# Adding b2 with the residual load of a decoder layer's feed-forward, in place of products with ones

## The reference, cut to what matters

```
def _quant_per_tensor(x):
    scale = jnp.maximum(jnp.max(jnp.abs(x)), MIN_RANGE) / QP
    return (_ste_round(x / scale), scale)

def _qlinear(x2d, w, b):
    xq, sx = _quant_per_tensor(x2d)
    wq, sw = _quant_per_tensor(w)
    out = jnp.matmul(xq, wq.T) + b[None, :]
    return out * (sw * sx)

h = _qlinear(x.reshape(-1, D), w1, b1)
h = jax.nn.gelu(h, approximate=False)
o = _qlinear(h, w2, b2)
x = x + o
```

## Time and profile before

| what | us |
|---|---|
| median of 3 runs | 1654.87 |
| lowest and highest | 1651.92, 1656.31 |
| profiled execution, its own time | 1657.15 |
| its span, first to last instruction | 1655.3 |
| second pass: scale of h known, to the last add_residual's start | 1549.5 to 1650.55 |

### The profile page before, as it was taken

How to read it: one execution, slowest core, us unless ns; L and a number is a source line. 1 busy time by engine, 2 the same in 40 slices (tenths; PEclk the granted TensorE clock), 3 DMA queues, 4 the chain that set the end, 5 groups by cost and what they waited for, 6 DMA issues and landing times.

```text
span 1655.3 us, 52293 instructions
## 1 busy us (share of the span) xinstructions
PE 1546.7 (93%) x15938; PEld 1228.1 (74%) x15946; DVE 1460.6 (88%) x6188; ACT 1216.4 (73%) x2497; POOL 1074.7 (65%) x1168
## 2 busy tenths in 40 slices
PE   6689999999999999999999999999999999779897
PEld 5568888888888788888888888888888887542465
DVE  4779999999999999999999999999999997669876
ACT  4767777777777777777777777777777776469875
POOL 3467777777777777777777777777777777642000
PEclk9789999999999999999999999999999999889999
DMA  6000000000000000000000000000000000246154
GB/s 213 1 18 29 29 29 29 29 26 24 27 29 29 29 29 29 29 22 23 26 29 26 24 29 29 29 29 29 29 29 29 29 29 17 90 103 151 39 178 166
DMA packets 92292, 74.67 MB, mean 45 GB/s; under 512 B 20832, under 2 KB 91744, under 8 KB 92256
## 3 DMA queue, kind: packets, MB, share of 16 engines
q1 hardware_dynamic: 91296, 74.08, 14.5%
q10 hardware_dynamic: 960, 0.13, 0.1%
HBM read 45.36 MB, written 25.17 MB: 43 GB/s over the span
## 4 chain that ended last, share of the span: by engine, by line
PE 40%; DVE 35%; issue 12%; ACT 6%; DMA 3%; POOL 2%; DVEq 1%; SPq 1%; ACTq 0%; POOLq 0%
PE banks L124 10%; PE banks L127 8%; PE banks L128 8%; DVE scores L1379 6%; DVE tile_max L2118 4%; PE banks L906 3%; DVE sparse_in L1450 3%; DVE heads_t_half L1401 2%; PE banks L926 2%; DVE xn L1334 2%; DMA x_in<-in_x_dram 2%; DVE left L1431 2%; PE banks L798 2%; PE banks L2022 2%; DVE g_t_half L1355 2%
## 5 line engine op out<-in xcount | busy, mean ns | idle before, releaser
L646 POOL TENSOR_TENSOR shifted<-scores,score_max 128x512 f32<-128x512 f32 x256 | 266.8, 1048 | 200.4 <-DVE score_max L1379 195.7
L652 POOL TENSOR_TENSOR exp_t<-exp_copy,exp_t 128x512 f16<-128x512 f32 x256 | 303.9, 1187 | 81.0 <-ACT exp_copy L1168 78.5
L1379 DVE CUSTOM_DVE_ANT_0 scores<-banks,mask 128x128 f32<-128x128 f32 x1024 | 232.7, 285 | 6.5 <-PE banks L906 2.9
L638 POOL TENSOR_TENSOR v_nat<-kv_copy,v_nat 128x512 f16<-128x512 f32 x128 | 149.3, 1167 | 44.4 <-ACT kv_copy L1146 44.4
L1143 ACT ACTIVATE q_t<-banks 128x512 f16<-128x512 f32 x128 | 77.1, 603 | 131.4 <-PE banks L128 131.1
L926 PE MATMUL banks<-ident,shifted 128*128 128x128 f32 x1024 | 153.6, 278 | 10.5 <-ACT exp_copy L1168 6.9
L1166 ACT ACTIVATE exp_t<-banks 128x512 f16<-128x512 f32 x256 | 152.6, 596 | 5.7 <-PE banks L116 2.9
L1168 ACT ACTIVATE exp_copy<-banks 128x512 f32<-128x512 f32 x256 | 155.3, 607 | 0.0
L1146 ACT ACTIVATE kv_copy<-banks 128x512 f32<-128x512 f32 x252 | 149.8, 595 | 0.0
L638 POOL TENSOR_TENSOR k_t<-kv_copy,k_t 128x512 f16<-128x512 f32 x124 | 144.2, 1163 | 0.0
L114 PE MATMUL banks<-v_nat,exp_t 128*128 128x66 f16 x1024 | 121.9, 195 | 7.9 <-POOL exp_t L652 3.2
(11 more groups left out here) (276 smaller groups left out, 5117.4 us busy)
## 6 DMA issues: line engine op xcount, KB each, us to landing
x_in<-in_x_dram SPq DMA_DIRECT2D x32, 256.0 KB, 2.7
ctx_in<-in_ctx_dram SPq DMA_DIRECT2D x32, 256.0 KB, 2.6
x_residual<-x SPq DMA_DIRECT2D x64, 128.0 KB, 1.7
x_normalised<-normed SPq DMA_DIRECT2D x32, 256.0 KB, 2.1
shared<-x_normalised SPq DMA_DIRECT2D x8, 1024.0 KB, 7.0
shared<-x_residual SPq DMA_DIRECT2D x16, 512.0 KB, 3.7
out_dram<-shared SPq DMA_DIRECT2D x16, 512.0 KB, 2.9
mask<-in_fside_Bx1xSxS_dram SPq DMA_DIRECT2D x64, 64.0 KB, 2.0
```

Source lines behind the costliest of these rows:

```text
L638: pool.tensor_tensor(hilo(dst, *at)[LO], src, hilo(dst, *at)[HI], ALU.subtract).then_inc(kv_split, 1)
L646: pool.tensor_tensor(shifted[:, q % 2], scores[:, q % 2], score_max[:, q % 2, :].unsqueeze(2).to_broadcast([P, QUAD, P]), ALU.subtract).th ...
L652: pool.tensor_tensor(exp_t[:, q % 2, LO], exp_copy[:, q % 2], exp_t[:, q % 2, HI], ALU.subtract).then_inc(exp_split, 1)
L1379: op = dve.tensor_tensor_reduce(scores[:, q % 2, h, :], sc_bank(q)[:, tile(h)], mask[:, b, :], 1.0, NEG, ALU.add, ALU.max, score_max[:, q ...
```

## The change

`split_b2`, the tensors `ones` and `b2_parts`, and the 32 matmuls of L2028 are removed. The last product of each slice in a half closes the sum, and VectorE waits for `stepped` in place of `acc_full`. GpSimd computes `b2_scaled` = b2 * s once, after the scale of h is known. `reload(n)` on SyncE's queue no longer loads the residual: it copies `b2_scaled` into the four places of the slot, from SBUF to SBUF. When that has landed (`b2_put`), GpSimd's queue issues the load of the residual with `accum_op=ALU.add`, so the slot then holds x2 + b2 * s, and this load's landing is what `again_loaded` counts. The transfer reads the slot, adds, and writes it.

```
-            if back and not front:
-                ffn_of["split_b2"](pool)
...
-    b2_parts = sb("b2_parts", [P, 2, D], BF16)
-    ones = sb("f_ones", [P, P], BF16)
+    b2_scaled = sb("b2_scaled", [P, D])
...
         def reload(n):
-            sp.dma_start(x_again[:, n % 2], x2_halves[half_of(n)]).then_inc(again_loaded[n % 2], 16)
-
-        sp.wait_ge(b2_ready, 3)
+
+            sp.dma_start(x_again[:, n % 2], b2_scaled[:].unsqueeze(1).to_broadcast([P, HB, D])).then_inc(b2_put[n % 2], 16)
+
+        sp.wait_ge(b2_ready, 1)
         reload(0)
         reload(1)
...
+        half_of = lambda n: 2 * SEQUENCE[n // 2] + n % 2
+        pool.wait_ge(b2_loaded, 16)
+        pool.wait_ge(scale_step, 6)
+        pool.tensor_scalar(b2_scaled[:], keep["b2_row"][:], both[:, 1:2], None, ALU.mult).then_inc(b2_ready, 1)
+        for n in range(HALVES):
+            pool.wait_ge(b2_put[n % 2], 16 * (n // 2 + 1))
+            pool.dma_start(x_again[:, n % 2], x2_halves[half_of(n)], accum_op=ALU.add).then_inc(again_loaded[n % 2], 16)
...
-                               keep["w2_q"][:, t, :], start=(t == 0 and b % 2 == 0), stop=False, skip_group_check=True)
+                               keep["w2_q"][:, t, :], start=(t == 0 and b % 2 == 0), stop=(t == ET - 1), skip_group_check=True)
             mm.then_inc(stepped, 1)
-            if t == ET - 1:
-                for b in (0, 2):
-                    mm = pe.matmul(acc_bank(half, b), ones[:], b2_parts[:].rearrange("p n d -> p (n d)"),
-                                   start=False, stop=True, skip_group_check=True)
-                mm.then_inc(acc_full, 1)
 
         pe.wait_ge(h_ready, UNITS)
-        pe.wait_ge(b2_ready, 3)
...
         def add_residual(n):
-            dve.wait_ge(acc_full, n + 1)
+            dve.wait_ge(stepped, (n + 1) * ET)
             dve.wait_ge(again_loaded[n % 2], 16 * (n // 2 + 1))
```

More of the change, by code:

```diff
@@ L1744, in feed_forward @@
     x_again = shared[:, ET * TOK:].rearrange("p (n b d) -> p n b d", n=2, b=HB)
-    b2_left = x_again[:, 0, 0:2, :]
-    b2_high = x_again[:, 0, 2, 0:D // 2].bitcast(BF16)
-    b2_mid = x_again[:, 0, 3, 0:D // 2].bitcast(BF16)
     NAT = 2
@@ L1761, in feed_forward @@
     u_full, h_ready, h_seen = sem("u_full"), sem("h_ready"), sem("h_seen")
-    b2_step, b2_ready = sem("b2_step"), sem("b2_ready")
+    b2_ready, b2_put = sem("b2_ready"), [sem("b2_put0"), sem("b2_put1")]
     u2_full, h2_ready, h2_rounded = sem("u2_full"), sem("h2_ready"), sem("h2_rounded")
     taken_act, taken_dve = sem("taken_act"), sem("taken_dve")
-    stepped, acc_full, acc_free = sem("stepped"), sem("acc_full"), sem("acc_free")
+    stepped, acc_free = sem("stepped"), sem("acc_free")
     again_loaded = [sem("again_loaded0"), sem("again_loaded1")]
@@ L1943, in sync @@
             sp.wait_ge(stored[n], 16 * HALVES // 2)
[L1945 to L1960, removed]
     def gpsimd(pool):
@@ L2152, in feed_forward @@
     return {"sync": sync, "gpsimd": gpsimd, "tensor": tensor, "scalar": scalar, "vector": vector, "load_weights": load_weights,
-            "load_first": load_first, "split_b2": split_b2, "prime": prime, "weight_peak": weight_peak, "peak_spread": peak_spread, "weight_row": weight_row, "weight_one": weight_one, "weight_spread": weight_spread,
+            "load_first": load_first, "prime": prime, "weight_peak": weight_peak, "peak_spread": peak_spread, "weight_row": weight_row, "weight_one": weight_one, "weight_spread": weight_spread,
             "quantise": quantise, "weight_transpose": weight_transpose, "weight_take": weight_take}
```

## The result

| | before | after |
|---|---|---|
| median of the runs, us | 1655.57 | 1699.9 |
| lowest and highest, us | 1651.92, 1656.31 | 1698.15, 1700.06 |
| span of the profiled execution, us | 1655.3 | 1698.3 |

A forecast was written before the change was run, and what follows sets the result against it. TensorE, partly with VectorE, bounded the pass; the residual slot's loop would take over at 15.35 us a cycle. Seven cycles add 25.4 us, less 0.4 for the earlier start: 1654.87 + 25 = 1680 us, range 1655 to 1711.

The forecast's parts named there:

- the forecast's own case: Second feed-forward pass: the slot's loop becomes the bound, adding load about 4.5 to 8.3 us; 1669 to 1692 us, chance 0.58.
- The bound: Second pass: TensorE and VectorE bound cycles of 12.06 and 11.72 us; afterwards the residual slot's loop does, at 15.35.
- The signs: Profile after: additions wait 2 to 4 us a half for the adding load, 15 us apart per slot; DMA share about 0.8.
- What is removed: The 32 products with ones on TensorE: 4.2 to 6.9 us gained if nothing else changed, 5.5 taken.
- Added once: At the pass's start: scaling b2 0.39 us, then copy and adding load into the first slots, covered by 1.3 us.
- The copy, P: Every half: copy of b2 into the slot, issue to landing, 3.7 us taken, from 2.9 to 4.2.
- The adding load, X: Every half: adding load of the residual, issue to landing, 6.6 us as load 3.7 plus second pass 2.9.
- My 0.5 us a cycle for overlap: Slot's cycle: 0.5 us allowed because the two slots' transfers often overlap on the DMA engines.
- The sum: Slot's cycle 1.43 + 3.12 + 3.7 + 6.6 + 0.5 = 15.35 us; seven take 107.5, not 82.03: +25.0.
- Rival one: GpSimd's issue of the load held up by a pair of VectorE's roundings, 2.48 us: cycle 17.8, 1699 us, chance 0.2.
- Rivals two and three: Two: adding costs nothing more, X 3.7, 1654 us, chance 0.1. Three: P + X under some 6.7, 1649 us, chance 0.12.

The follow-up runs named there:

- The third slot: The changed kernel with a third residual slot in a free part of the ring of hidden units, so a slot's loop has three halves: 1679.18 us, 1.0142.

## Why the prediction was right, and where its size was off

Forecast 1680 us, range 1655 to 1711, slower with 0.77; measured 1699.9, slower. It lies in the range, but above the 1669 to 1692 of the forecast's own case. By its steps:

- **The bound.** Right: the slot's loop takes over, the additions wait for the adding load, TensorE for the takes behind them. The third slot gives back half of the loss. The signs came as written: DMA share 0.76 (about 0.8 said), and the wait for a late load was 4.2 us in the mean (2 to 4 said).
- **What is removed.** Mis-sized: 5.5 us taken, 3 measured, since only one of two 0.43 us a cycle lies on the path. It did not matter to the sum, which counted only 0.4 us of it, at the start.
- **Added once.** Mis-sized: the scaling took 2.82 us, not 0.39, beside VectorE's roundings, and the first load 7.1, not 6.6, so the start was not covered. The addition of half 0 began at 1563.61 and that of half 1 at 1570.17, 2.1 us later than the 1568.1 in my sum. But when VectorE did the scaling, in 0.35 us, the median stayed, so leaving it out gives nothing back.
- **The copy, P.** This is the largest miss: 3.7 taken, 5.5 measured. It lands in 3.9 beside plain loads, so 1.6 us of it is the other slot's adding load on the same DMA engines. By the means of slot 1 it took 6.0 us until GpSimd's issue, 2.3 more than taken. My 0.5 us a cycle for overlap was for all transfers together.
- **The adding load, X.** 6.6 taken as load plus store, 7.1 measured as median, 7.3 as the mean of slot 1. That adding costs a second helping of DMA work was right: 3.65 us of all engines against 2.06. Part of the agreement is luck, since 6.6 left out GpSimd's queue (4.6 for a plain load, not 3.7) and its hold-up.
- **The sum.** A cycle of slot 1 took 17.6 us, not 15.35: +2.3 for the copy, +0.7 for the load, -0.3 for the store (2.84, not 3.12), -0.5 for the overlap counted apart. Seven cycles took 123.3 us, not 107.5 (+15.8), and the start +2.1: 17.9 of the 18.0 us between the forecast span of 1680.3 and the 1698.3 measured.
- **Rival one** gave 1699, the time measured, but as 2.48 us on X in every load. The runs show the hold-up, some 0.5 us of X in the mean, and the rest of that time was made by P: its number was right by luck. The rule of the Trainium skill, page SBUF — State Buffer, section Who interferes with whom, also says that whichever of the two engines issues first has the shared port pair for its whole instruction, and the other blocks. The trace agrees for DMA issues beside tensor_scalar (1.28 alone, 3.70 beside roundings), and for VectorE behind GpSimd's arithmetic (1.22 to 3.38).
- **Rivals two and three** fall: adding cost 2.3 us of landing, and P + X was 12.6 us, not below 6.7. The fit of the Trainium skill, page DMA: Bandwidth & Descriptors, section Anatomy of one DMA, gives an estimate of 3.2 us for 512 KB; the runs show 4.6 for the plain load and 7.1 for the adding one, and they decide.

## What to carry to other kernels

Before a transfer is put into a buffer's loop, sum the loop: here 8.25 us of 12 left 3.7, and two transfers in a row needed 12.6. Price each transfer beside the ones that it will overlap with, since the added traffic of one slot lengthened the landings of the other by more than the adding itself was mis-sized. And before work is removed from an engine, ask whether its place is what costs: in this kernel, moving the two matmuls from the end of a half to its start gained 4 us (2.3 to 5.6), and leaving them out 3 (1.5 to 4.5).

## What the runs showed of the hardware that I had not expected

- An adding load of 512 KB in 1 KB rows took 3.65 us of all 16 DMA engines and 528 packets, a plain one on the same queue 2.06 us and 144 packets.
- GpSimd's issue of a transfer took at least 0.75 us for the plain form and 1.28 for the adding one, and up to 3.70 beside VectorE's roundings.
- A copy of 512 KB from SBUF to SBUF landed in 3.2 us with no adding load beside it, and in up to 7.0 us with one.
- A GpSimd tensor_tensor of 128 x 1024 took 2.3 to 3.9 us, and a VectorE tensor_scalar of 2048 columns beside it 3.38 us where it is 1.22 alone: both lose.
